# Turning the softmax shift columns with four 32x32 transposes on VectorE in place of a TensorE product

## The reference

```
theta = theta_w @ x                      (32 x 1024, per image)
phi   = pool2(phi_w @ x)                 (32 x 256)
beta  = softmax(theta^T phi, over the 256)
g     = pool2(g_w @ x)                   (128 x 256)
o_in  = g @ beta^T                       (128 x 1024)
v     = gamma * (o_w @ o_in) + x
out   = v + toeplitz(filter of 27 taps, circular, middle 0) @ v      (over the 256 channels)
```

## Time and profile before

| | |
|---|---|
| median of 3 runs | 278.06 us |
| profiled execution, its own time | 277.08 us |
| its span, first to last instruction | 275.4 us |
| granted TensorE clock | 1.00 of full speed throughout |
| PE busy / PEld busy | 268.0 us (97%) / 212.5 us (77%) |
| DVE busy | 239.1 us (87%) |
| ACT busy | 243.1 us (88%) |
| POOL busy | 152.2 us (55%) |
| L1015 PE, the shift product | 15 of 221 ns, and its loads 15 of 94 ns |
| L770 DVE, the multiplications with the mask | 30 of 679 ns |

### The profile page before, as it was taken

How to read it: one execution, slowest core, us unless ns; L and a number is a source line. 1 busy time by engine, 2 the same in 40 slices (tenths; PEclk the granted TensorE clock), 3 DMA queues, 4 the chain that set the end, 5 groups by cost and what they waited for, 6 DMA issues and landing times.

```text
span 275.4 us, 4412 instructions
## 1 busy us (share of the span) xinstructions
PE 268.0 (97%) x1210; PEld 212.5 (77%) x1210; DVE 239.1 (87%) x402; ACT 243.1 (88%) x532; POOL 152.2 (55%) x78
## 2 busy tenths in 40 slices
PE   7899999999999999999999999999999999999894
PEld 3477778787878878787887878888787888878683
DVE  4999899898989989898998989899898989989843
ACT  3999899998999999898999989999898989988662
POOL 5486646574664657456564755656475466636000
PEclk9999999999999999999999999999999999999999
DMA  7977085582838558183765718466572846235034
GB/s 201 262 201 207 27 231 167 182 212 94 187 126 231 167 169 217 82 198 129 219 179 169 212 60 209 146 211 187 167 171 85 224 148 200 45 152 94 14 141 154
DMA packets 17380, 44.57 MB, mean 162 GB/s; under 512 B 2654, under 2 KB 3578, under 8 KB 16122
## 3 DMA queue, kind: packets, MB, share of 16 engines
q1 hardware_dynamic: 16826, 44.26, 55.8%
q10 hardware_dynamic: 544, 0.20, 0.3%
HBM read 17.45 MB, written 16.78 MB: 124 GB/s over the span
## 4 chain that ended last, share of the span: by engine, by line
PE 91%; ACT 3%; DVE 2%; DMA 2%; issue 0%; SPq 0%
PE psY L968 10%; PE psY L947 7%; PE psY L948 7%; PE psY L949 7%; PE psV L1086 5%; PE psY L1086 5%; PE psY L1070 5%; PE psV L1070 5%; PE psV L947 3%; PE psX L1024 3%; PE psV L948 3%; PE psV L949 3%; PE psV L1091 3%; PE psX L1008 3%; PE psY L1054 3%; PE psV L1054 3%
## 5 line engine op out<-in xcount | busy, mean ns | idle before, releaser
L446 POOL TENSOR_TENSOR prob_lo<-prob,prob_hi 128x1024 fp32r<-128x1024 f32 x30 | 72.3, 2411 | 63.4 <-ACT prob L525 36.2
L439 POOL TENSOR_TENSOR x_lo<-x_raw,x_hi 128x1024 fp32r<-128x1024 f32 x30 | 72.0, 2401 | 34.3 <-ACT x_hi L492 32.0
L492 ACT CAST x_hi<-x_raw 128x1024 fp32r<-128x1024 f32 x30 | 31.5, 1050 | 4.7 <-PE psY L1054 4.4
L514 ACT ACTIVATE psX<-psX,neg_max 128x256 f32<-128x256 f32 x60 | 26.8, 446 | 3.1 <-DVE neg_max L752 2.5
L514 ACT ACTIVATE psZ<-psZ,neg_max 128x256 f32<-128x256 f32 x60 | 27.4, 470 | 0.0
L690 DVE TENSOR_TENSOR thetaphi<-psY,thetaphi_rest 64x512 f32<-64x512 f32 x30 | 20.5, 682 | 2.0
L947 PE MATMUL psY<-x_hi,g_hi_w 128*128 128x512 f32 x56 | 22.2, 396 | 0.0
L948 PE MATMUL psY<-x_lo,g_hi_w 128*128 128x512 f32 x56 | 22.2, 396 | 0.0
L949 PE MATMUL psY<-x_hi,g_lo_w 128*128 128x512 f32 x56 | 22.1, 396 | 0.0
L696 DVE TENSOR_TENSOR theta_aug<-thetaphi,theta_aug 32x512 fp32r<-32x512 f32 x30 | 20.5, 683 | 0.9
L683 DVE TENSOR_REDUCE phi_pool<-thetaphi 32x128 f32<-32x512 f32 x30 | 20.2, 675 | 1.0
(11 more groups left out here) (185 smaller groups left out, 761.3 us busy)
## 6 DMA issues: line engine op xcount, KB each, us to landing
x_raw<-x SPq DMA_DIRECT2D x30, 512.0 KB, 5.0
out<-y SPq DMA_DIRECT2D x15, 1024.0 KB, 4.0
x_edge<-x_hi SPq DMA_DIRECT2D x64, 104.0 KB
x_edge<-x_lo SPq DMA_DIRECT2D x32, 104.0 KB
x_raw<-x SPq DMA_DIRECT2D x4, 256.0 KB, 4.7
out<-y SPq DMA_DIRECT2D x4, 256.0 KB, 2.5
band_rev<-ring SPq DMA_DIRECT2D x2, 128.0 KB, 7.0
proj_raw<-proj_wT ACTq DMA_DIRECT2D x1, 128.0 KB, 4.8
```

Source lines behind the costliest of these rows:

```text
L439: nc.gpsimd.tensor_tensor(x_lo[:, par, :, cols], x_raw[:, par, :, cols], x_hi[:, par, :, cols].bitcast(F32), ALU.subtract).then_inc(x_lo_r ...
L446: nc.gpsimd.tensor_tensor(prob_lo[:, h], prob[:, h], prob_hi[:, h].bitcast(F32), ALU.subtract).then_inc(prob_lo_ready, 1)
L492: nc.scalar.copy(x_hi[:, par, :, cols], x_raw[:, par, :, cols]).then_inc(x_hi_ready[h], 1)
L514: last = nc.scalar.activation(tiles[:, t, :], tiles[:, t, :], ACT.Exp, bias=neg_max[:, col:col + 1], accum_out=exp_sum[:, col:col + 1])
```

## The change

The shift product on TensorE goes, in the steady images and in image 0. In its place VectorE turns `shift_parts` by four 32x32 transposes: partitions 0 to 31, 32 to 63, 64 to 95 and 96 to 127 each become 32 columns of the same 32 partitions of a PSUM region. For this `shift_parts` is widened to 32 columns (the last 16 are zero). The multiplications keep their size of 16x512; their mask is now 16x8, read with each element repeated 128 times along the columns, in place of 16x8x128. `ident_r`, the rounded identity, goes with its cast on VectorE. The order on VectorE changes as well: the transposes and both multiplications now stand right behind `shifts`, ahead of the copy out of PSUM; in image 0 `shift_rows0(0)` goes ahead of `sum_thetaphi(0, 1, 0)` and `shift_rows0(1)` ahead of `pool_phi(0, 1, 0)`.

```diff
-        own_tile = sb("own_tile", [SHIFT_ROWS, 2 * NT, P])
+        own_tile = sb("own_tile", [SHIFT_ROWS, 2 * NT])
-        shift_parts = sb("shift_parts", [P, 2 * NT, 2], F32R)
+        shift_parts = sb("shift_parts", [P, SQUARE // 2, 2], F32R)
-        shift_ps = psZ[0:SHIFT_ROWS, 0, 0:P]
+        shift_turned_ps = psZ[:, 1, 4 * NT:4 * NT + TURNED]
...
-            def shift_rows(i, par, h):
-                dve.wait_ge(shift_rows_done, from_second(1, i, par, 1))
-                row = shift_ps[:, :].rearrange("q (o n) -> q o n", o=1).broadcast_to([SHIFT_ROWS, NT, P])
-                rows = theta_aug[R_SHIFT:K_AUG, par, :].rearrange("q (t n) -> q t n", n=P)
-                tiles = slice(h * NT, (h + 1) * NT)
-                nc.vector.tensor_tensor(rows[:, tiles, :], row, own_tile[:, tiles, :],
-                                        ALU.mult).then_inc(shift_rows_ready, 1)
+            def turn_shifts(turned):
+                parts = shift_parts[:, :, :].rearrange("p t s -> p (t s)").bitcast(F32)
+                for q in range(0, P, SQUARE):
+                    last = nc.vector.transpose(turned[0:SQUARE, q:q + SQUARE], parts[q:q + SQUARE, :])
+                return last
+            def spread_shifts(turned, par, first, end):
+                rows = theta_aug[R_SHIFT:K_AUG, par, :].rearrange("r (t n) -> r t n", n=P)
+                row = turned[0:SHIFT_ROWS, :].rearrange("r (o n) -> r o n", o=1).broadcast_to([SHIFT_ROWS, end - first, P])
+                own = own_tile[:, first:end].rearrange("r (t o) -> r t o", o=1).broadcast_to([SHIFT_ROWS, end - first, P])
+                return nc.vector.tensor_tensor(rows[:, first:end, :], row, own, ALU.mult)
+            def shift_rows(i, par):
+                dve.wait_ge(shift_parts_ready, from_second(1, i, par, 1))
+                turn_shifts(shift_turned_ps).then_inc(shift_turned_ready, 1)
+                dve.wait_ge(shift_turned_ready, from_second(1, i, par, 1))
+                for h in range(2):
+                    spread_shifts(shift_turned_ps, par, h * NT, (h + 1) * NT).then_inc(shift_rows_ready, 1)
...
             shifts0(0)
+            shift_rows0(0)
             sum_thetaphi(0, 1, 0)
-            shift_rows0(0)
             pool_g(0, 1, 0)
             shifts0(1)
             w2_high()
+            shift_rows0(1)
             pool_phi(0, 1, 0)
-            shift_rows0(1)
...
             shifts(0, 1)
-            shift_rows(0, 1, 0)
+            shift_rows(0, 1)
             out_of_psum(0, 0, 1, 0)
-            shift_rows(0, 1, 1)
...
                 shifts(ni, npar)
+                shift_rows(ni, npar)
                 out_of_psum(i, par, 0, 0)
-                for h in range(2):
-                    shift_rows(ni, npar, h)
...
-            def shifts_to_rows(i, par):
-                pe.wait_ge(shift_parts_ready, from_second(1, i, par, 1))
-                nc.tensor.matmul(shift_ps, shift_parts[:, :, :].rearrange("p t s -> p (t s)"), ident_r[:],
-                                 start=True, stop=True).then_inc(shift_rows_done, 1)
```

More of the change, by code:

```diff
@@ L50, in attention_then_channel_filter @@
     K_AUG = R_SHIFT + SHIFT_ROWS
+    SQUARE = 32
+    TURNED = P
     REACH = 13
@@ L121, in attention_then_channel_filter @@
         w2_ps = turn_ps[1][:, 0:C]
-        shift_ps = psZ[0:SHIFT_ROWS, 0, 0:P]
+        shift_turned_ps = psZ[:, 1, 4 * NT:4 * NT + TURNED]
         ln_sum_ps = psZ[:, 1, 0:2 * NT]
         shift_sum_ps = psZ[:, 1, 2 * NT:4 * NT]
-        first_shift_ps = [ps[0:SHIFT_ROWS, 0, 0:P] for ps in scores_ps]
+        first_shift_turned_ps = [ps[:, 1, 4 * NT:4 * NT + TURNED] for ps in scores_ps]
         first_ln_sum_ps = [ps[:, 1, 0:NT] for ps in scores_ps]
@@ L198, in attention_then_channel_filter @@
         shift_parts_ready = sem("shift_parts_ready")
[L199 removed]
+        shift_turned_ready = sem("shift_turned_ready")
         shift_rows_ready = sem("shift_rows_ready")
@@ L390, in own_tiles @@
             def own_tiles():
-                nc.gpsimd.memset(own_tile[:], 1.0).then_inc(own_tile_ready, 1)
+                first = own_tile[:]
+                nc.gpsimd.memset(first, 1.0).then_inc(own_tile_ready, 1)
                 pool.wait_ge(own_tile_ready, 1)
-                nc.gpsimd.affine_select(out=own_tile[:], in_=own_tile[:], compare_op=ALU.is_ge, fill=0.0, base=0,
-                                        pattern=[[-2, 2 * NT], [0, P]], channel_multiplier=1).then_inc(own_tile_ready, 1)
+                nc.gpsimd.affine_select(out=first, in_=first, compare_op=ALU.is_ge, fill=0.0, base=0,
+                                        pattern=[[-2, 2 * NT]], channel_multiplier=1).then_inc(own_tile_ready, 1)
                 pool.wait_ge(own_tile_ready, 2)
-                nc.gpsimd.affine_select(out=own_tile[:], in_=own_tile[:], compare_op=ALU.is_ge, fill=0.0, base=1,
-                                        pattern=[[2, 2 * NT], [0, P]], channel_multiplier=-1).then_inc(own_tile_ready, 1)
+                nc.gpsimd.affine_select(out=first, in_=first, compare_op=ALU.is_ge, fill=0.0, base=1,
+                                        pattern=[[2, 2 * NT]], channel_multiplier=-1).then_inc(own_tile_ready, 1)
+                pool.wait_ge(own_tile_ready, 3)
             def x0_low(h, t):
@@ L835, in shift_rows0 @@
             def shift_rows0(h):
+                dve.wait_ge(shift0_parts_ready, h + 1)
+                turn_shifts(first_shift_turned_ps[h]).then_inc(shift0_turned, 1)
                 if h == 0:
                     dve.wait_ge(own_tile_ready, 3)
[L839 to L844, removed]
+                dve.wait_ge(shift0_turned, h + 1)
+                spread_shifts(first_shift_turned_ps[h], 0, h * NT, (h + 1) * NT).then_inc(shift_rows_ready, 1)
             def w2_high():
@@ L987, in g_transposed @@
                 if is_first(i, par):
-                    pe.wait_ge(ident_r_ready, 1)
+                    pe.wait_ge(ident_ready, 1)
                 elif not is_second(i, par):
@@ L1139, in fold_weights @@
                 last.then_inc(w2_done, 1)
-            def shifts_to_rows0(h):
-                pe.wait_ge(ident_r_ready, 1)
-                pe.wait_ge(shift0_parts_ready, h + 1)
-                nc.tensor.matmul(first_shift_ps[h], shift_parts[:, :, :].rearrange("p t s -> p (t s)"), ident_r[:],
-                                 start=True, stop=True).then_inc(shift0_rows_done, 1)
             pe.wait_ge(idle_operand_ready, 1)
```

18 lines of the change are left out of this document (3 added, 15 removed).

## The result

The changed kernel takes 278.46 us (median of 15 runs, 278.03 to 282.0); the kernel before, run beside it, took 276.72 (15 runs, 276.53 to 278.37). The ratio is 1.0068, 95% interval [1.0049, 1.0088]: about 0.7% slower. The forecast was 278.7 with 0.6 for no difference by the bound of 0.5%, so the time was met, and the sign only by the side chance of 0.3. That the time was met is luck in part: the median of three runs on which the forecast stood was 1.3 us higher than that of these 15, and the change costs 1.7 us by the medians and 1.9 by the ratio, 1.1 to 1.3 more than the +0.6 forecast. The two errors cancelled.

The account below looks back on a forecast made before the run. TensorE was taken to bound the steady images, VectorE image 0, its end and the passage into the last. +2.62 - 13 x 0.17 + 0.18 = +0.6 us gave 277.7, plus 0.98 for the median 278.7; range 277.0 to 282.3.

Parts of the forecast that it names:

- The set of transposes, 0.93 us: On VectorE: four transposes of 0.20 us, with four gaps of 0.03, take 0.93 us; bounds 0.56 and 1.24.
- rival B: On VectorE: the transposes overlap, a set takes 0.56 us, the sum is -0.9 us, time 277.2; chance 0.12.
- rival C: On VectorE: the mask read 128 times per element runs at half rate, 0.54 us more per multiplication, time 295; chance 0.05.
- Image 0, +1.75: In image 0: two transpose sets ahead of `gT_low` make the attention product and everything behind it 1.75 us later.
- Rival D: Image 0 costs little and TensorE's gain remains: sum -2.0 us, time 276.1; chance 0.09.
- End of image 0, 1.0 more: The copy moved behind both multiplications makes the g projection's load 2.77 us later, 1.0 of it new.
- Tail, +0.18: Passage into the last image: with the copy ahead of it and the idle time gone, `gT_low` starts 0.18 us later.
- TensorE's 0.17 us in each steady image: On TensorE: 0.11 us for the product plus 0.06 us waiting for the rows, gained in 13 steady images, 2.2 us.
- further on in the image the lag goes: Steady images, VectorE: casts L710 wait for GpSimd's `prob_lo` anyway, so a start 0.1 us later costs 0.
- Cover left, 0.07 us: Steady images: VectorE's first sum ends 0.07 us before TensorE's `theta_phi` needs it, so each transpose may take 0.22 us.
- Rival A: Transposes of 0.28 us exceed the cover and TensorE waits in steady images: sum +5.0 us, time 283.1; chance 0.24.
- What the product's removal gives: On TensorE in steady images: removing the shift product, its 128 columns and an uncovered load, saves 0.11 us per image.

Follow-up runs that it names:

- image0_product: Changed kernel with image 0 as before (both shift products on TensorE, old VectorE order there), transposes from image 1 on; 277.58 us, ratio 1.0017 to the kernel before.
- copy_first: Changed kernel with the copy that the g projection waits for, at the end of image 0, moved between the two multiplications; 278.43 us.
- no_product_order: Kernel before without the shift product in images 1 to 15 and with both multiplications ahead of the copy out of PSUM; 274.4 us, period 16.05.
- lockfree: Changed kernel with the first of the two phi casts written as a reduction over a one-element axis; 277.75 us, ratio 1.0021 to the kernel before.
- no_product: Kernel before without the shift product in images 1 to 15, repeated shift sums standing in for the rows; 276.55 us, period 16.18.
- order_only: Kernel before, shift product kept, with both multiplications ahead of the copy out of PSUM in images 1 to 14; 276.73 us, ratio 0.9991.

## Why the prediction came out as it did

The steps in the order of the prediction:

- *The set of transposes, 0.93 us*: right to the hundredth, by two small errors. Each takes 0.215 instead of 0.20, and the gap is 0.013 instead of 0.03 (start to start 0.2275). Within a set no transpose starts before its predecessor ends, so rival B, the overlap, is false (only the first of image 0's second set, behind `w2_high`, starts 0.08 ahead of its predecessor's end), and the held start that the Trainium skill states in "VectorE: DVE Perf Modes", "Two Vector instructions with no wait between them" is what the trace shows here; by overlap the set would be 0.56. The estimate of 0.21 from the same page's "The three transpose paths" agrees with the 0.215.
- *The mask, rival C*: false, 679 ns before and 678 after.
- *Image 0, +1.75*: right. 1.81 from the common start; `image0_product` gives 1.80 back. Rival D is dead with it.
- *End of image 0, 1.0 more*: 0.82 between the two loads. From the end of `shifts` to the load it is 2.01 us before and 3.02 after, the 1.0 that was worked out; but `shifts` itself was only 1.62 late from the common start, not the 1.75 forecast. `copy_first` shows that 0.59 of it is the copy's place alone.
- *Tail, +0.18*: 0.17.
- *TensorE's 0.17 us in each steady image*: this term was mis-sized, 0.11, and 13 times 0.06 is the 0.8 us by which the sum was short (0.6 forecast, 1.4 seen). Two steps of the prediction made it so.
  - The gross gain is 0.14, by `no_product_order`. The product's part, 0.11, is nearly right: by the loads it is 0.10. The wait for the rows, 0.06, is 0.05 on average. It was read against the 0.11 us between two loads at the end of image 0, and with the rows there early the distance is 0.11 in every second image only, and 0.135 to 0.157 in the others; what the load waits for there stays open.
  - 0.03 to 0.04 was lost again, to the step "further on in the image the lag goes: the casts L710 take 0.96 for two because the first one stands until GpSimd's `prob_lo` ends ... a start 0.1 later changes nothing there". That step failed. It took GpSimd's end for a fixed point. In the earlier trace rows ScalarE does release that `prob_lo`, and so it does in every steady image of before; but VectorE's `theta_low`, the other thing it waits for, left it only 0.06 and 0.22 us of margin in turn, and the change makes it later than that. From there on GpSimd ends later when VectorE is later, and the lag is handed back to VectorE instead of being absorbed. Two independent cuts, at the cast and at GpSimd's wait, bring the period to 16.04 and 16.05.
- *Cover left, 0.07 us*: near the truth, as long as the ring is cut. The sum must end 0.05 us ahead of the load that waits for it. In `lockfree` it ends 0.16 to 0.19 ahead in five steady images, so 0.10 to 0.14 is left, and `shifts` ends 3.72 to 3.75 us ahead of that load, where 3.70 was forecast. In the changed kernel `shifts` ends only 3.61 us ahead of it where TensorE waits. The cover was eaten by `shifts` coming late, through the ring, and not by the set. Rival A had this signature, TensorE idle ahead of L968's second half, but not its cause: the transposes stayed under 0.22. The sign named for it could not tell the two apart.
- *What the product's removal gives* was booked as TensorE's own, whatever the order. `no_product` says otherwise: 0.01. The term came near the truth because the change moves the copy as well.

What stays open: in every second image GpSimd starts 0.22 us behind the end of `theta_low` and in the others 0.08. The alternation of 16.15 and 16.00 goes with this 0.14 and went when the first `prob_lo` no longer waited; before has the same 0.22 and 0.08 ahead of its second `prob_lo`. What takes the 0.14 wasn't found.

## What to carry to other kernels

Before a lag is written off at an instruction that stands for another engine, follow that engine's start through all that it waits for, and not only through what came last: if the lagging engine is among it, what counts is the margin (here 0.06 us in every second image), and a lag beyond the margin comes round again. An instruction taken off the bounding engine gives nothing while another engine's answer to that engine's own earlier work ends last. And an edit that is nearly free in a steady image must be priced apart at the head of the pipeline, where the receiving engine has no idle time: here 2.6 us once against 0.11 us 13 times.

## What the runs showed of the hardware

- A 32x32 float32 transpose on VectorE from SBUF to PSUM takes 0.215 us, and four that start at partitions 0, 32, 64 and 96 follow at 0.2275.
- An operand whose elements are read 128 times each costs a multiplication nothing: 678 ns for 512 columns.
- A plain cast of 32x256, 0.29 us by itself, stands until GpSimd's tensor_tensor ends: begun at 154.19 it ends at 154.90, 0.145 after GpSimd's 154.755. The same move written as a reduction takes 0.41 and doesn't stand.
- TensorE's clock can drop in the last image. Stretches of `order_only` (us, busy us and instructions of each engine, granted clock, DMA):

```profile
255.00:258.00 3.00, 3.00 (x15) 2.41 (x14) 1.85 (x6) 1.62 (x8) 0.00 (x0) 1.00 0.00 0
258.00:261.00 3.00, 1.69 (x8) 0.76 (x6) 2.31 (x4) 2.59 (x5) 0.00 (x0) 1.00 0.00 0
261.70:265.10 3.40, 3.40 (x10) 2.62 (x9) 1.35 (x2) 2.04 (x3) 0.00 (x0) 0.50 0.66 257
266.00:270.00 4.00, 4.00 (x19) 3.25 (x18) 0.90 (x2) 1.01 (x2) 0.00 (x0) 1.00 0.00 0
```

The granted clock falls from 2.4 to 1.2 GHz behind a stretch in which TensorE was busy 1.69 of 3.00 us. That alone doesn't decide it: the changed kernel, ahead of the same products, was busy 1.59 of 3.00 us and kept its clock:

```profile
259.98:262.98 3.00, 1.59 (x6) 0.76 (x6) 2.61 (x6) 2.56 (x5) 0.00 (x0) 1.00 0.00 0
263.00:266.40 3.40, 3.40 (x16) 2.73 (x16) 1.23 (x1) 2.72 (x3) 0.00 (x0) 1.00 0.77 308
```

In `order_only` the stretch from the last maxima to the end took 24.63 us instead of the 22.81 of before. In `image0_product` 5 of 12 runs have a mean clock of 0.991 or 0.992 against 0.997 to 1.00, and 278.0 to 278.4 us (spans 276.3 to 276.7), where six of the other seven took 276.7 to 277.2. Where in those five the clock fell, no trace shows; if at the end, some of what a faster middle gains is lost there by chance.
